# Wide attention on one core: the query first in a unit, attended values ahead of the 16-bit halves, the next head's keys and values in two units

## What is computed

```
qh = _split_heads(jnp.einsum('bnq,qi->bni', x, Wq))
kh = _split_heads(jnp.einsum('bmc,ci->bmi', context, Wk))
vh = _split_heads(jnp.einsum('bmc,ci->bmi', context, Wv))
sim = jnp.einsum('hid,hjd->hij', qh, kh) * SCALE
mean = jnp.mean(sim, axis=-1, keepdims=True)
sim = (sim - mean) * ATTN_MATRIX_SCALE + mean
attn = jax.nn.softmax(sim, axis=-1)
out = jnp.einsum('hij,hjd->hid', attn, vh)
...
return jnp.einsum('bni,iq->bnq', out, Wout) + bout
```

## Time and profile before

| | |
|---|---|
| median of 3 runs | 3515.93 us (3515.02 to 3516.57) |
| profiled execution | 3514.8 us, span of its profile 3513.1 us |
| wide attention's scores | 719 to 1841 us of the span |
| TensorE busy over the span | 3065.2 us (87%) |
| VectorE, ScalarE, GpSimd busy | 2178.1, 2025.1, 925.2 us |
| transposes in the stage | 512, two for each of 256 tiles |

### The profile page before, as it was taken

One profiled execution on the slowest core, in us unless ns is written; L12 is line 12 of the kernel. 1 busy time (PEld: TensorE's weight loads), 2 busy tenths in 40 slices (PEclk: granted clock), 3 DMA queues, 4 the chain that ended last, 5 costly groups with the idle time before them and its releaser, 6 DMA issues. The chain is left out here.

```text
span 3513.1 us, 88734 instructions
## 1 busy us (share of the span) xinstructions
PE 3065.2 (87%) x34175; PEld 2480.8 (71%) x34175; DVE 2178.1 (62%) x5141; ACT 2025.1 (58%) x3673; POOL 925.2 (26%) x800
## 2 busy tenths in 40 slices
PE   8999999578888888888886799899899899688699
PEld 6888888456666666666665678678678788454498
DVE  5777777555545555555552577677677677565643
ACT  5777777466556656556561467567567567342344
POOL 3444444254544445445450000000000000111010
PEclk9999999789999999999998899999999999898799
DMA  2212121356666666667676201101101100452300
GB/s 73 68 54 66 55 66 55 86 101 122 125 113 119 128 117 122 123 119 126 119 154 208 99 32 38 62 32 38 63 32 38 56 32 32 137 173 72 94 25 24
DMA packets 654282, 298.66 MB, mean 85 GB/s; under 512 B 550171, under 2 KB 628464, under 8 KB 650944
## 3 DMA queue, kind: packets, MB, share of 16 engines
q1 hardware_dynamic: 628672, 242.43, 30.7%
q10 hardware_dynamic: 25344, 52.44, 4.2%
HBM read 127.53 MB, written 33.03 MB: 46 GB/s over the span
## 5 line engine op out<-in xcount | busy, mean ns | idle before, releaser
L1094 POOL TENSOR_TENSOR wide_parts<-wide_prob,wide_parts 128x1024 f16<-128x1024 f32 x256 | 547.1, 2137 | 585.2 <-ACT wide_parts L1282 583.9
L1380 DVE TENSOR_REDUCE wide_row_max<-wide_score 128x1 f32<-128x1024 f32 x256 | 313.5, 1225 | 389.0 <-PE wide_score L1128 385.4
L1128 PE MATMUL wide_score<-wide_kT,wide_qT 128*128 128x512 f32 x1536 | 407.1, 401 | 92.7 <-DVE wide_qT L1347 74.1
L1270 ACT ACTIVATE wide_prob<-wide_score,wide_neg_max 128x1024 f32<-128x1024 f32 x256 | 285.5, 1115 | 347.7 <-DVE wide_neg_max L1383 347.2
L1128 PEld LDWEIGHTS wide_score<-wide_kT,wide_qT 128*128 128x128 f32 x1536 | 276.9, 189 | 166.8 <-DVE wide_qT L1347 83.8
L641 ACT ACTIVATE mask_prob<-mask_prob,mask_row_min 128x256 f32<-128x256 f32 x512 | 232.0, 503 | 161.5 <-DVE mask_row_min L730 161.5
L1282 ACT ACTIVATE wide_parts<-wide_prob 128x1024 f16<-128x1024 f32 x256 | 270.7, 1058 | 26.0 <-ACT wide_prob L1270 10.8
L2168 DVE TENSOR_REDUCE cell_row_max<-cell_score 128x8 f32<-128x512 f32 x192 | 131.2, 684 | 189.8 <-PE cell_score L1836 187.9
L1821 PE MATMUL cell_score<-cell_w,cell_node 128*128 128x256 f32 x1152 | 165.4, 306 | 38.6 <-DVE cell_node L2115 23.6
L1155 PE MATMUL wide_misc<-wide_w_qo_split,wide_oT 128*128 128x256 f32 x768 | 121.7, 294 | 84.6 <-DVE wide_oT L1366 84.4
L1821 PEld LDWEIGHTS cell_score<-cell_w,cell_node 128*128 128x128 f32 x1152 | 160.9, 213 | 48.4 <-DVE cell_node L2115 21.6
(11 more groups left out here) (336 smaller groups left out, 6895.5 us busy)
## 6 DMA issues: line engine op xcount, KB each, us to landing
cell_w_stage<-cell_weights ACTq DMA_DIRECT2D x24, 1280.0 KB, 5.5
mask_ctx<-in_ctx SPq DMA_DIRECT2D x32, 512.0 KB, 4.0
ctx_ctx<-in_ctx SPq DMA_DIRECT2D x32, 512.0 KB, 4.3
mask_mask<-in_mask_BxS_ik SPq DMA_DIRECT2D x32, 256.0 KB, 4.2
wide_probT<-wide_parts SPq DMA_TRANSPOSE x512, 3.1
mask_x_ln<-in_x SPq DMA_DIRECT2D x32, 128.0 KB, 2.1
mask_x_res<-in_x SPq DMA_DIRECT2D x32, 128.0 KB, 2.1
x_after<-mask_x_res ACTq DMA_DIRECT2D x32, 128.0 KB, 1.7
```

The costliest lines, as they stand in the source:

```text
L1094: pool.tensor_tensor(parts[:, s % 2, LO, :], prob[:, s % 2, :], parts[:, s % 2, HI, :], ALU.subtract).then_inc(part_lo, 1)
L1128: mm = pe.matmul(score[:, s % 2, half * 512:(half + 1) * 512], qT[:, u_par, a, s * P:(s + 1) * P], kT[:, par, b, half * 512:(half + 1) * 5 ...
L1270: act.activation(prob[:, s % 2, :], score[:, s % 2, :], ACT.Exp, bias=neg_max[:, s % 2:s % 2 + 1], scale=SHARP, accum_out=row_sum[:, u_par ...
L1380: dve.tensor_reduce(row_max[:, one], score[:, s % 2, :], AX.X, ALU.max).then_inc(max_found, 1)
```

## The change

Four things are moved; no arithmetic changes.

1. TensorE makes the next unit's query at the front of turn 0, ahead of the scores, where it was at the end of turn 0. ScalarE and VectorE copy it in turn 0 (ScalarE before the leading half) and no longer in turn 1.
2. In turn 3 the second half of the attended values goes ahead: on ScalarE before `take_leading`, on VectorE before `find_max`, behind the first `add_output`.
3. The next head's keys products are made in turns 0 and 1 of unit n = 6 (new edge "keys"), the values products in turns 0 and 1 of unit n = 7, all in the bank `misc`. The weights are split in turn 2 of unit n = 6.
4. The inner loop has two passes instead of three; units n = 5 and n = 6 are written out.

```diff
--- before.py
+++ after.py
@@ -879,7 +879,7 @@
     misc_ps = mem.ps("misc", [P, 512])
     pv_banks = (pv_ps, turn_ps[0][:, 0:HALF])
     query_ps = turn_ps[1]
-    kv_banks = (misc_ps, misc_ps, query_ps, query_ps)
+    KV_AT = {"keys": {0: 0, 1: 1}, "close": {0: 2, 1: 3}}
     x_all = mem.sb("x_all", [P, NBLK * SUB, D])
     xnT = mem.sb("xnT", [P, 2, DH, TOK], F32R)
@@ -965,9 +965,11 @@
         def head(pair, par, last):
-            with eng.Fori(0, NBLK // 2 - 1) as i:
+            with eng.Fori(0, NBLK // 2 - 2) as i:
                 for j in (1, 2):
                     unit(pair, par, i * 2 + j, j % 2, "mid")
+            unit(pair, par, NBLK - 3, 1, "mid")
+            unit(pair, par, NBLK - 2, 0, "mid" if last else "keys")
             unit(pair, par, NBLK - 1, 1, "last" if last else "close")
             if not last:
                 unit(pair + par, 1 - par, 0, 0, "open")
@@ -1162,6 +1164,11 @@
             before = 1 - par if edge == "open" else par
             behind = 1 - par if edge == "close" else par
             for s in range(SUB):
+                if s == 0 and edge != "last":
+
+                    if edge == "close":
+                        pe.wait_ge(w_lo, h + 2)
+                    query(behind, 0 if edge == "close" else n + 1)
                 if s < 2 or edge != "last":
                     pe.wait_ge(exp_done, g + s + 1)
@@ -1179,25 +1186,18 @@
                 elif edge != "first":
                     hf, part = (s + 1) // 2, (s + 1) % 2
                     attend(u - 1, 1 - u_par, hf, before, part)
-                if edge == "close":
+                if edge in KV_AT and s < 2:
+                    i = KV_AT[edge][s]
                     if s == 0:
-                        pe.wait_ge(w_loaded[behind], (pair + par + 1) * W_LOADS)
+                        pe.wait_ge(w_loaded[1 - par], (pair + par + 1) * W_LOADS)
                         pe.wait_ge(y_added, u * 2 - 2)
-                    pe.wait_ge(kv_lo, (h + 1) * KV + s)
-                    kv(behind, s, kv_banks[s][:, :])
+                    pe.wait_ge(kv_lo, (h + 1) * KV + i)
+                    kv(1 - par, i, misc_ps[:, :])
                 if edge != "first" and s >= 2:
+                    if edge in KV_AT and s == 2:
+                        pe.wait_ge(kv_lo, (h + 1) * KV + KV_AT[edge][1] + 1)
                     pe.wait_ge(y_added, u * 2 - 4 + s)
                     project_out(u * 2 - 4 + s, s - 2, before)
-                if s == 0 and edge != "last":
-
-                    if edge == "close":
-
-                        pe.wait_ge(w_lo, h + 2)
-                    if edge == "open":
-
-                        pe.wait_ge(kv_lo, (h + 1) * KV)
-                    query(behind, 0 if edge == "close" else n + 1)
-
         pe.wait_ge(c_loaded, 16)
         for c in range(CT):
@@ -1287,19 +1287,24 @@
             for s in range(SUB):
                 if s + 1 < SUB:
                     exp(u, u_par, s + 1)
+                elif edge != "last":
+                    exp(u + 1, 1 - u_par, 0)
+                if s == 0 and edge != "last":
+                    query_hi(u + 1, 1 - u_par)
+                if edge != "first" and s == 3:
+                    output_hi(u * 2 - 1, 1)
+                if s + 1 < SUB:
                     take_leading(u, s + 1)
                 elif edge != "last":
-                    exp(u + 1, 1 - u_par, 0)
                     take_leading(u + 1, 0)
-                if s == 0 and edge == "close":
+                if edge != "first" and s == 1:
+                    output_hi(u * 2 - 2, 0)
+                if edge in KV_AT and s < 2:
+                    i = KV_AT[edge][s]
+                    kv_hi_part(1 - par, i, misc_ps[:, :], (h + 1) * KV + i + 1)
+                if edge == "keys" and s == 2:
                     act.wait_ge(w_loaded[1 - par], (pair + par + 1) * W_LOADS)
                     weights_hi(h + 1, 1 - par)
-                if edge != "first" and s % 2 == 1:
-                    output_hi(u * 2 - 2 + s // 2, s // 2)
-                if s == 1 and edge != "last":
-                    query_hi(u + 1, 1 - u_par)
-                if edge == "close":
-                    kv_hi_part(1 - par, s, kv_banks[s][:, :], (h + 1) * KV + s + 1)
         for i in range(CT * (KEYS // 512)):
             act.wait_ge(c_turned, i + 1)
@@ -1392,20 +1397,22 @@
             g = u * SUB
             block_before = NBLK - 1 if edge == "open" else n - 1
             for s in range(SUB):
+                if edge != "first" and s == 3:
+                    add_output(u * 2 - 2, 0, block_before, 1 - u_par)
+                    output_lo(u * 2 - 1, 1)
                 if s < 2 or edge != "last":
                     find_max(g + s + 2, s)
-                if edge != "first" and s == 3:
-                    add_output(u * 2 - 2, 0, block_before, 1 - u_par)
                 if s + 1 < SUB:
                     invert_sum(u, u_par, s + 1)
-                if s == 0 and edge == "close":
+                if s == 0 and edge != "last":
+                    query_lo(u + 1, 1 - u_par)
+                if edge != "first" and s == 1:
+                    output_lo(u * 2 - 2, 0)
+                if edge in KV_AT and s < 2:
+                    i = KV_AT[edge][s]
+                    kv_lo_part(1 - par, i, misc_ps[:, :], (h + 1) * KV + i + 1)
+                if edge == "keys" and s == 2:
                     weights_lo(h + 2, 1 - par)
-                if edge != "first" and s % 2 == 1:
-                    output_lo(u * 2 - 2 + s // 2, s // 2)
-                if s == 1 and edge != "last":
-                    query_lo(u + 1, 1 - u_par)
-                if edge == "close":
-                    kv_lo_part(1 - par, s, kv_banks[s][:, :], (h + 1) * KV + s + 1)
                 if edge != "first" and s == 3:
                     add_output(u * 2 - 1, 1, block_before, 1 - u_par)
```

## The result

The changed kernel takes 3331.02 us (median of 4 runs, 3327.4 to 3336.33) where the kernel before took 3516.25 (4 runs, 3515.02 to 3522.4) beside it: a ratio of 0.9471, interval 0.9454 to 0.9488, or 185.2 us less. The forecast was 3320 with a range of 3302 to 3374. The profiled execution is the longest of the four, 3336.33 with a span of 3334.6.

What follows compares the result with a forecast made beforehand. TensorE, nearest to full, was held by two waits in each middle unit. Gains of 132.8 + 22.6 + 37.8 + 3 = 196.2 us from 3514.8 give 3318.6; the median, 1.1 above, is about 3320, whole range 3302 to 3374.

Steps and rivals of the forecast that it cites:

- both waits: TensorE's middle unit: 1.48 us for the query's low half, 1.76 for the attended values' low half; both predicted to go.
- the walk: One middle unit followed engine by engine in the new order: 13.62 us, smallest margin 0.6 us before the second projection.
- the change of head: Keys and closing units together: 33.9 us instead of 39.3, 5.4 a head, 37.8 for seven; 3 to 6.5 possible.
- middle units, 40: Wide attention's middle units shorten from 16.94 to 13.62 us, 3.32 each, 132.8 us in all.
- opening units, 7: First unit of each new head loses both waits and its wait for new values: 7 x 3.23 = 22.6 us.
- first two units and last: Units at the stage's ends, with other VectorE work or fewer turns: 3 us gained together.
- two jumps back: Jumps of the loop over pairs of heads, one showing a 3.68 us TensorE gap, stay as they were.
- I give 0.2 us for that: Keys unit, turn 2: weights copies push the second output half to about when it is wanted; charged 0.2 us.
- 1: Rival: part of the wait before the second projection remains, 0.7 us a unit, 40 us, 3360; chance 0.18.
- 2: Rival: the second projection's wait stays whole, only 1.58 us a unit won, 3426 us; chance 0.07.
- 3: Rival: code supply; inner loops' jumps stall like the outer one, 44 us given back, 3364; chance 0.04.
- 4: Rival: denser transposes land later and bind the unit; at 7 us landing, 3584 us, slower than before; chance 0.03.

Runs made afterwards that it cites:

- The undone halves: Changed kernel with the second attended half in turn 3 put back behind the 16-bit halves: both engines 3448.45 us, ScalarE alone 3363.77, VectorE alone 3449.67.
- The repeat: The changed kernel run again with no edit: 3328.17 us, ratio 0.9478 to the kernel before.
- the one undone: Changed kernel with only VectorE's order of turn 3 undone (low half behind the maximum and the addition): 3449.67 us.
- the other, undone alone: Changed kernel with only ScalarE's order of turn 3 undone (high half behind the leading half): 3363.77 us.

## Why the prediction was right, and where a term was not

The mechanism came as forecast: both waits are gone from the middle units, for the reasons that the walk gave, and each comes back when its part is undone. The step that failed is the pricing of the change of head, 28.0 us where 37.8 was forecast; smaller misses on both sides leave the sum 8.6 us short.

The stage runs from the first query (714.68 before, 716.98 after) to the last store of its residual (1859.5 and 1674.2): 1144.8 and 957.2 us, 187.6 less where 196.2 were forecast. By the terms of the sum:

| term | forecast | measured |
|---|---|---|
| middle units, 40 | 132.8 | 40 x 3.275 = 131.0 |
| opening units, 7 | 22.6 | 7 x 3.17 = 22.2 |
| keys and closing units, 7 | 37.8 | 7 x 4.00 = 28.0 |
| first two units and last | 3 | 5.8 |
| two jumps back | 0 | 1.3 |
| one wait for a transpose | 0 | -0.7 |

The middle and opening rows are means of all such units from query to query, those behind a jump back and the one wait for a transpose left out: the middle ones took 16.91 and take 13.64. The single unit of 16.94 from which the forecast was made is 0.03 above their mean, which is 1 of the 1.8 us that this term was high.

**The middle unit.** Laid end to end from rows of before it was 13.62, and it is 13.63 to 13.69 in every one but the two behind a jump back. That the sum meets it so closely is in part luck: the query takes 1.37 where 1.48 was taken, and the four scores 1.37, 1.48, 1.48 and 1.40 where four of 1.40 were taken, so 0.11 too much and 0.13 too little nearly cancel. The walk by which each engine is early enough held at its tight place, the second output half: 0.86 to spare against 0.6. The undone halves show the two parts it named, the leading copy and the maximum, and that either alone would have brought a wait back. It charged nothing for a denser TensorE; in the windows of 50 us from 750 to 1650 the granted clock is 1.00, but for the two with a jump back (0.93 and 0.97).

**The change of head, the mis-sized term.** "I give 0.2 us for that" was the step: the weights' copies in turn 2 of the keys unit cost 1.03, because VectorE's took 2.22 where the same one took 0.69 before; the prediction walked the turn without a duration for it. Moving them away gave exactly that back. The same subtraction had run at full speed before the change, at a time when GpSimd had nothing to do; VectorE's and GpSimd's timeline of before:

```profile
840.22 2.14 POOL L1094 TENSOR_TENSOR wide_parts<-wide_prob,wide_parts 128x1024 f16<-128x1024 f32 x1 [1.15 <-ACT wide_parts L1282]
843.04 0.69 DVE L1347 TENSOR_TENSOR wide_w_qo_split<-wide_w_qo,wide_w_qo_split 128x512 fp32r<-128x512 f32 x1
...
847.63 2.13 POOL L1094 TENSOR_TENSOR wide_parts<-wide_prob,wide_parts 128x1024 f16<-128x1024 f32 x1 [5.26 <-ACT wide_parts L1282]
```

The second part is the price of a keys product: 1.5 was taken, 1.70 it is. The product itself takes only 1.32 (811.75 to 813.07), but the scores behind it take 1.78 to the next group (813.07 to 814.85) instead of 1.48, and the attend ahead 1.32 instead of 1.24. A values product is 1.71 and 0.08, 1.79 for the 1.75 taken. Together: 13.64 + 3.41 + 1.03 = 18.08 and 13.64 + 3.58 = 17.22, 35.3 for the 33.9 of the forecast; 1.4 x 7 is the 9.8 that are short. The 4.0 a head lies within the 3 to 6.5 that the forecast allowed.

**The rest of the distance.** 9.8 from the change of head, 1.2 from the other terms the other way, and outside the stage this one execution is 2.3 later ahead of it and 6.8 longer behind it: 187.6 - 2.3 - 6.8 = 178.5, which is 3514.8 - 3336.3. The repeat does not show the 6.8 (1655.1 from the last store to the end, before 1653.6), so it need not be an effect of the change. The forecast's own range is mis-added by 2: 3320 less 7 and 8 is 3305, not 3303.

**The rivals.** 1 and 2 are ruled out by the list of waits: no middle unit waits for an output half. Of 3, the inner jumps cost TensorE nothing, and the outer ones stayed about what they were, 6.0 and 4.7 us after 6.2 and 5.8, with the slow products behind them, one of them here:

```profile
976.84 2.92 PE L1122 MATMUL wide_turn<-wide_xnT,wide_w_qo_split 128*128 x6 [2.89 <-issue]
979.56 2.76 PE L1130 MATMUL wide_score<-wide_kT,wide_qT 128*128 128x512 f32 x6
```

Of 4, the sign is there: a transpose lands after 3.3 (median, 3.1 in the earlier trace rows), and GpSimd waits for one 53 times, 65.4 us in all. It is covered in the middle units, for TensorE waited for a transpose once, 0.5 us. But much of the cover is gone: from the landing of a half's last transpose to its attend the median was 7.6 us and is 3.1 (first half of a unit) and 3.8 (second). At three of seven changes of head the first attend of the new head's values comes 0.24 to 0.34 us behind that landing (854.67, 1095.56 and 1334.6), where before no such margin at a change of head was under 5. The prediction had the opening unit wanting it "several us later"; this is the tightest place of the whole stage, and the one wait of 0.5 is there, at 1095.56.

## What to carry to other kernels

When a unit repeats, lay its bounding engine end to end from rows, then walk every other engine once round in the new order: here that gave the unit to 0.02 us, in part because two errors cancelled, and the smallest margin of the walk named the place where the next bound appeared. Walk the units at the change of head as carefully, for their margins are smaller. A copy moved from a place where a neighbour engine is idle to one where it is busy has to be priced beside that neighbour, not by its old duration, when all its operands lie in SBUF. When two engines hand on one result, undo the order on each alone before crediting either: here the one undone brought back the whole 113 us and the other, undone alone, 31.

## What the runs showed that was not expected

**VectorE beside GpSimd.** The 128x512 subtraction with both operands in SBUF takes 0.69 us alone and 2.22 beside GpSimd's 2.15 us remainder, ending half a microsecond after it wherever inside it starts. The query's low half is the same operation and size with one operand in a PSUM bank, and keeps its time in all 64 instances, of which 60 lie wholly inside a remainder (874.71 is within 873.50 to 875.65). The changed kernel's tile view:

```profile
L1352 DVE TENSOR_TENSOR wide_qT<-wide_turn,wide_qT x64: 671/692/692, 720.6 to 1643.4; 128x512 fp32r<-128x512 f32 x64
```

The Trainium skill (SBUF — State Buffer, Who interferes with whom) has a rule for it: VectorE's second read port is GpSimd's only one, so an instruction of VectorE that reads two operands from SBUF and one of GpSimd that reads SBUF exclude each other for their whole length. The trace agrees, with 2.22 against 0.69 and the end always 0.54 or 0.55 behind the remainder's. By that rule, as an estimate, the weights' copies could be held for up to the remainder's 2.15, where 0.2 was given.

**A later stage's time that hangs on code written out ahead of it.** With the pair loop written out, the next stage is about 7 us shorter in both such kernels (795.7, against 801.5 to 806.8 in the ten profiles with the loop); with the inner loop out as well it is 799.9, closer to the ten. That the 7 us come with the edit is shown by the two. What carries it, such as where that stage's code comes to lie, was not tried and stays open.

**Scores behind a keys product.** They take 1.78 instead of 1.48, behind a values product 1.47. Why the one slows them and the other does not was not settled.
